# First cross attention: the logarithm of the sums ahead of the turned copies, the scaling between maximum and distances

## The reference

```python
scores = qk / sqrt(8)                     # (b, h, q, 77); mean_sim uses its mean
max_sim, entropy = scores.max(-1), var(softmax(scores))
log_t = clip(mlp(stack([mean_sim, max_sim, entropy])), log 0.1, log 10)
attn = softmax(qk / (2 exp(log_t)))       # the second softmax
out = attn @ V; return out @ Wo.T + bo
```

## Time and profile before

| | us |
|---|---|
| median of 3 runs (1824.58 to 1828.66) | 1826.06 |
| the profiled execution | 1836.28 |
| its span | 1834.6 |

### The profile page before, as it was taken

The page is one execution under the profiler, slowest core; times in us unless marked ns, Lnnn a source line. Parts: engine busy times, 40 slices in busy tenths (PEclk is TensorE's granted clock), DMA queues, the critical chain, the costliest instruction groups (busy, mean ns, idle before and its releaser), DMA issues. The chain is left out here.

```text
span 1834.6 us, 28890 instructions
## 1 busy us (share of the span) xinstructions
PE 1630.5 (89%) x10524; PEld 956.3 (52%) x10524; DVE 1260.3 (69%) x1701; ACT 1202.9 (66%) x2569; POOL 481.8 (26%) x402
## 2 busy tenths in 40 slices
PE   5999999999999973889788798999999999789975
PEld 2343444444443431666665544666666667466654
DVE  2778777777777767888925555666666667488854
ACT  3787887787787752777882256565656566377754
POOL 2111011111101124766740001222222222155530
PEclk9999999999999985888995589999999999799997
DMA  3000001000000011000000000000000000000001
GB/s 132 1 12 1 1 6 25 1 0 0 0 0 1 0 38 38 8 5 8 2 2 0 1 1 1 1 1 1 1 1 1 1 1 1 8 8 8 2 1 46
DMA packets 30530, 16.99 MB, mean 9 GB/s; under 512 B 8545, under 2 KB 29247, under 8 KB 30399
## 3 DMA queue, kind: packets, MB, share of 16 engines
q1 hardware_dynamic: 27710, 10.52, 2.2%
q10 hardware_dynamic: 2688, 4.72, 0.7%
HBM read 13.14 MB, written 2.10 MB: 8 GB/s over the span
## 5 line engine op out<-in xcount | busy, mean ns | idle before, releaser
L2252 POOL TENSOR_TENSOR self_probs<-self_probs,self_rz 128x1024 f32<-128x1024 f32 x64 | 121.3, 1896 | 469.4 <-DVE self_rz L2283 469.4
L558 POOL TENSOR_SCALAR gru_decay<-gru_zgate 128x512 f32<-128x512 f32 x96 | 75.2, 783 | 561.1 <-ACT gru_zgate L509 535.0
L2227 ACT ACTIVATE self_probs<-self_scores,self_neg 128x128 f32<-128x128 f32 x512 | 179.2, 380 | 20.2 <-DVE self_neg L2278 20.2
L417 PE MATMUL gru_gate<-gru_xn,gru_whg 128*128 128x512 f32 x384 | 182.5, 598 | 3.5 <-DVE gru_xn L605 3.5
L421 PE MATMUL gru_hid<-gru_xn,gru_whg 128*128 128x512 f32 x384 | 180.5, 592 | 0.0
L1386 ACT ACTIVATE x_pt<-x_turned 77x512 f32<-77x512 f32 x256 | 137.3, 585 | 64.5 <-PE x_turned L1283 63.1
L429 PE MATMUL gru_out<-gru_y,gru_wo 128*128 128x512 f32 x384 | 178.2, 599 | 0.7 <-DVE gru_y L635 0.7
L1283 PE MATMUL x_turned<-const_ident,x_probs 128*77 128x128 f32 x1024 | 143.8, 285 | 23.2 <-POOL x_probs L1435 13.1
L1283 PEld LDWEIGHTS x_turned<-const_ident,x_probs 128*77 128x77 f32 x1024 | 116.4, 151 | 75.4 <-POOL x_probs L1435 27.6
L630 DVE SCALAR_TENSOR_TENSOR gru_ghid<-gru_hid,gru_half_c,gru_sighid 128x512 f32<-128x512 f32 x96 | 71.8, 748 | 108.2 <-ACT gru_sighid L510 108.1
L1492 DVE TENSOR_REDUCE x_m<-x_scores 128x16 f32<-128x1232 f32 x64 | 91.7, 1432 | 49.1 <-PE x_scores L1272 43.8
(11 more groups left out here) (440 smaller groups left out, 3518.4 us busy)
## 6 DMA issues: line engine op xcount, KB each, us to landing
gru_whg<-in_L_attn_Whg ACTq DMA_DIRECT2D x4, 768.0 KB, 8.4
x0e_ctx_in<-in_ctx SPq DMA_DIRECT2D x16, 154.0 KB
gru_xin<-in_x SPq DMA_DIRECT2D x8, 256.0 KB, 2.9
out<-moe_y SPq DMA_DIRECT2D x8, 256.0 KB
gru_wo<-in_L_attn_Wo ACTq DMA_DIRECT2D x4, 384.0 KB, 9.7
selfe_raw<-in_L_attn_Wq SPq DMA_DIRECT2D x1, 512.0 KB, 4.2
selfe_raw<-in_L_attn_Wk SPq DMA_DIRECT2D x1, 512.0 KB, 5.4
selfe_raw<-in_L_attn_Wv SPq DMA_DIRECT2D x1, 512.0 KB, 6.6
```

What stands on the lines that cost most here:

```text
L417: mm(ps_gate[n % 2][:, :], whg[:, l, k, DI + c * P:DI + (c + 1) * P], xn[u][:, k, :], start=(k == 0), stop=(k == KH - 1))
L2227: last = f(probs[n % 2][:, a, jj, :], ps_s[:, a, jj * T:(jj + 1) * T], ACT.Exp, bias=neg[n % 2][:, a, jj:jj + 1], accum_out=z[n % 2][:, a, ...
L2252: pool.tensor_tensor(probs[n % 2][:, :, :, :], probs[n % 2][:, :, :, :], whole, ALU.mult).then_inc(pn_ready.sem, 1)
```

## The change

Two steps of the first cross attention's iteration change their place. logs(n-10) goes ahead of turn(n-8) parts 0 and 1; only ACT takes part in logs, so on ACT the logarithm and the exponential of the sums come ahead of two copies. The distances become a step of their own, dist(n), behind scale(n-10); only DVE takes part in both, so on DVE the order for odd n goes from maximum, distances, scaling to maximum, scaling, distances. For even n DVE's order stays. PE's, POOL's and SP's order stays, no instruction is added or taken away, and every wait stays with its instruction. For `temper=False` the order is as before.

```diff
--- before.py
+++ after.py
@@ -1186,7 +1186,7 @@
                 ORDER += [("scale", n - LA, 0)] + place(n, 1, False) + place(n, 1, True)
                 continue
             ORDER += [("scores", n, 0), ("kbd", n + 1, 0), ("pre", n - LE, 0)]
-            ORDER += [("turn", n - LT, 0), ("turn", n - LT, 1), ("logs", n - LA - 1, 0), ("scale", n - LA - 1, 0)]
+            ORDER += [("logs", n - LA - 1, 0), ("turn", n - LT, 0), ("turn", n - LT, 1), ("scale", n - LA - 1, 0), ("dist", n, 0)]
             ORDER += [("divide", g - 4, 0)] * (r == 0)
             ORDER += place(n, 0, False) + place(n, 0, True)
             ORDER += [("soft", n, 0), ("sums", n - 1, 0)]
@@ -1195,7 +1195,7 @@
             ORDER += [("exp", n - LE, 0), ("attend", n - LA, 0)]
             ORDER += place(n, 1, False) + place(n, 1, True)
             ORDER += [("feat", g - 1, 0)] * (r == 0) + [("mean", g, 0), ("rate", g - 1, 0)] * (r == 2)
-        PER_SEQ = ("scores", "pre", "turn", "sums", "attend", "logs", "scale", "soft", "exp", "kbd", "weigh")
+        PER_SEQ = ("scores", "dist", "pre", "turn", "sums", "attend", "logs", "scale", "soft", "exp", "kbd", "weigh")
         ORDER = [s for s in ORDER if 0 <= s[1] < (B if s[0] in PER_SEQ else NG)]
         MISC = {}
         for kind, n, _ in ORDER:
@@ -1490,10 +1490,12 @@
                         dve.wait_ge(s_mm.sem, n + 1)
                         top = m[:, n, :].rearrange("p (r i) -> p r i", i=TILE4)
                         v.tensor_reduce(top, scored(), AX.X, ALU.max).then_inc(m_ready.sem, 1)
+                    if kind == ("dist" if temper else "scores"):
+                        top = m[:, n, :].rearrange("p (r i) -> p r i", i=TILE4)
                         dve.wait_ge(m_ready.sem, n + 1)
                         v.tensor_tensor(dist[:, n % RING, :, :].rearrange("p (r i) s -> p r i s", i=TILE4), scored(),
                                         top.unsqueeze(3).broadcast_to([P, TILE4, TILE4, S]), ALU.subtract).then_inc(d_ready.sem, 1)
-                    elif kind == "sums":
+                    if kind == "sums":
                         if n % GB == 0 and n:
                             dve.wait_ge(feat_ready.sem, n // GB)
                         dve.wait_ge(e1_ready.sem, n + 1)
```

## The result

| | before | after |
|---|---|---|
| median of 5 runs, us | 1828.66 | 1840.26 |
| lowest and highest, us | 1824.58, 1838.47 | 1831.87, 1844.96 |
| profiled execution and its span, us | 1836.28, 1834.6 | 1844.96, 1843.2 |
| mean granted clock | 0.930 | 0.925 |

The ratio of after to before is 1.0059, 95% interval 1.0032 to 1.0086. It was repeated with twelve runs of the change on another occasion: 1.0068 (1.0039 to 1.0097). The change makes the kernel about 11 us slower; forecast were +1.9 us and a range up to 1833. Runs of one and the same kernel spread: those of before lie mostly near 1824 or near 1834 us, the profiled one in the upper band, and what parts the bands no run here shows.

What follows compares the result with a forecast made beforehand. The prediction took a chain from engine to engine, not one full engine, as the bound. Distances +2.2 us and last scores -0.3 us gave +1.9 us, so 1826.06 + 1.9 = 1828.0 us, range 1820 to 1833.

Steps and rivals of the forecast that it cites:

- The bound: No engine fills a group; a chain across engines sets its length, twice through distances done, then ACT's `x_e`.
- The logarithm is free: On ACT, logarithm and exponential moved ahead of the copies take 0.82 us, fit into idle time and cost nothing.
- The distances 0.20 us later, 2.2 us in all: On DVE, distances behind the scaling start 0.20 us later in eleven odd iterations: +2.2 us, bounds 0 and +4.5.
- Attend earlier, on PE, "I put both at 0": Attend moves up 0.7 us in r = 1, some 1.4 in r = 3; gain put at 0 in both.
- Behind the last scores, -0.3 us: In iterations 33 to 41, without distances, only the logarithm moves; between 0 and -3.2 us, taken as -0.3 us.
- the clock falls lower or more often: Rival, chance 0.18: half clock may cover r = 0, +8.2 us on top of 1.9, 1836; one more stretch, 1829.8.
- The signs: Observations in the trace, named ahead, that would show the forecast right or wrong.
- "right": `x_dist` 1.6 to 1.9 us, `x_oT` 1.3 to 1.5 after `x_m`; no `x_oT` wait; longer `x_sq`, `x_dist` waits.
- "wrong": Full-clock groups under 30.0 us, DVE waiting for `x_rz` ahead of distances, or a group at 0.50 over 6.8 us.
- The range: Whole kernel: 1820 to 1833 us, meant to leave out most of PE-bound and the far end of clock lower.
- one case among five: Cases: forecast 0.58, PE the bound 0.12, clock lower 0.18, clock up 0.12, and no effect on the chain.

Runs made afterwards that it cites:

- the change with fill: The changed kernel plus five useless PE transposes per group in r = 2, ahead of the network's second and third layers: 1824.63 us, 0.9981 of before.
- run with r = 3 alone: The changed kernel with scaling ahead of distances on DVE only in r = 3, logarithm first everywhere: 1825.92 us, 0.9982 of before.

## Why the prediction was wrong

- *The bound* was read rightly: the chain runs through "distances done, ACT's `x_e`" in r = 1 and r = 3. Behind ACT's stretch in r = 1 and 2 it goes on through PE's attend and values, as the prediction says too, and there the price came. At full clock iterations 17 and 18 take 6.07 + 9.63 = 15.70 us in after and 6.92 + 8.58 = 15.50 in before, 0.20 more.
- *The logarithm is free*: right, and run alone it costs nothing that the runs can tell.
- *The distances 0.20 us later, 2.2 us in all*: right in size (0.21 and 0.22 us). The Trainium skill (VectorE: DVE Perf Modes, "The DRAIN you can't avoid") says that the next operation waits until the pipe is empty, and in the same place that one which is not held starts earlier. The prediction left the second part out, and it is the one that fits the row: the scaling started 0.08 us ahead of the maximum's recorded end (1.30 against 1.38).
- *Attend earlier, on PE, "I put both at 0"*: this step failed. It asked what releases ACT and who is next on the chain, and said rightly that nothing comes earlier. It did not ask what PE's clock does when the pause lands in the next iteration. In r = 1 the 0.7 us went into r = 2, whose idle time rose from 1.26 to 2.11 us, and there it brought stretches at half clock under attend and values. The four windows at half clock are 13.25 - 9.57 = 3.7, 12.07 - 9.63 = 2.4, 11.85 - 9.63 = 2.2, and 11.33 - 8.55 = 2.8 us over their full clock length (for n = 14 and 30 from the change with fill): 11.1 us, against 11.33 - 8.58 = 2.75 in before, 8.4 us more. With 5 x 0.20 for the distances of r = 1 that is 9.4, and the iterations with r = 1 and r = 2 are together 9.3 us longer. The others nearly cancel: r = 3 is 1.2 us shorter and r = 0 1.5 longer, since the stretches there fell differently. Together it is the 9.5 us between maximum 11 and 31; the medians say about 11.
- *Behind the last scores, -0.3 us*: it did not come. From the scaling of n = 31 to the last of the stage it is 51.19 us in before and 51.26 in after.
- *The rival "the clock falls lower or more often"* is the one that came, with 0.18. That its +8.2 and 1.9 add up to nearly the measured 11 is luck, since its place was wrong: it looked at r = 3 and the iteration with r = 0, the 1.61 us pause that was easiest to see. The run with r = 3 alone shows that that pause can be moved for nothing. As far as these runs go, what decides is the iteration that has pauses of its own and work of PE on the chain behind them.
- *The signs* named ahead did not part the cases. All those of "right" came: the starts on DVE (within 0.01 us), no wait for `x_oT`, a wait of 1.5 to 2.3 us for `x_sq` at n = 15, 19, 23 and 27, and longer waits of ACT for the distances, 38.0 us for 28.0 between 680 and 960 us. None of them looks at what time was lost. Of "wrong" one came, more than 6.8 us on end at half clock, at n = 14:

```profile
784.10:794.30 10.20, 10.12 (x95) 8.10 (x96) 5.36 (x11) 5.72 (x8) 2.47 (x3) 0.50 0.01 2
```

- *The range* had its upper end at 1833 because the clock's cost was taken as one case among five and mostly cut off.

## What to carry to other kernels

When a stall of PE is off the chain, moving it need not be free: look which pauses it joins, and whether the work behind them is on the chain, for that work may run at half clock. Where PE must wait anyway, a few transposes of no use in the pause can be worth more than the wait that was removed; in the kernel before, which had few such stretches, they gained nothing that the runs could tell. Moving one operation ahead of another on DVE costs what follows it only the start-to-start time of the moved one, here 0.33 us less 0.11 to 0.13 us of overlap gained, 0.21 to 0.22 us as measured.

## What the runs showed of the hardware

TensorE's granted clock fell from 2.4 to 1.2 GHz (1.00 to 0.50) behind pauses that are each short: 0.58, 0.62 and 1.04 us in iteration 22 of after, with work between them. In before, with 0.22 and 1.04 us there, it stayed up in four of five such iterations. But the pauses alone do not decide it. Iteration 18 of after has the same three, and attend behind them runs at full clock:

```profile
816.12 1.10 PE L1283 MATMUL x_turned<-const_ident,x_probs 128*77 128x128 f32 x8 [0.58 <-ACT x_probs L1376]
817.83 0.41 PE L1309 MATMUL x_misc<-x_g,x0e_w2T 128*128 128x64 f32 x2 [0.62 <-ACTq L1361]
819.28 0.41 PE L1313 MATMUL x_misc<-x_g,x0e_w3b 128*128 128x64 f32 x2 [1.04 <-ACTq L1366]
...
820.50 1.08 PE L1297 MATMUL x_out<-x_pt,x0e_vpad 77*32 77x128 f32 x32
```

What makes the difference between iterations 18 and 22 no run here shows. The Trainium skill (TensorE: Matmul & The Clock Gate, "Part 1: The HAM clock gate") has it that activity is what releases the throttle. The runs with fill agree: five short transposes, rows of 0.38 and 0.50 us that take 0.55 us off PE's idle time per group, moved the median by 15.6 us, and the same five in r = 0 did not help.
